# A decoder layer with a mixture of experts: VectorE's routing of the first two batches split in two, the rest of it moved to the end of a loop step

## The reference

```python
x = x + _layernorm(_L0_attn_ref(_layernorm(x), ...))     # 16 heads of 128, causal, rotary, gated keys and values
x = x + _layernorm(_L0_ffn_ref(_layernorm(x), ...))      # 8 experts, 2 per token, and a shared MLP
```

```python
logits = jnp.einsum('td,de->te', x_flat, router)         # 2048 tokens, 8 experts
topk_logits, sel = jax.lax.top_k(logits, K)              # K = 2
cw = jax.nn.softmax(topk_logits, axis=-1)
C = int(np.ceil(T * K / E * CAP_FACTOR))                 # 640 slots per expert
e_flat = sel.reshape(-1)
oh = jax.nn.one_hot(e_flat, E, dtype=jnp.int32)
pos_all = jnp.cumsum(oh, axis=0) - oh                    # how many earlier choices took the same expert
pos = jnp.take_along_axis(pos_all, e_flat[:, None], axis=1)[:, 0]
valid = pos < C
buf = jnp.zeros((E, C, d)).at[e_flat, safe_pos].set(x_flat[tok], mode='drop')
```

## Time and profile before

| | |
|---|---|
| median of the runs | 801.26 us (799.38 to 807.01) |
| profiled execution: its span | 801.3 us |
| granted TensorE clock, mean | 0.988 |
| TensorE busy | 746.7 us, 93% |
| VectorE busy | 599.3 us, 75% |
| GpSimd busy | 560.1 us, 70% |
| ScalarE busy | 500.0 us, 62% |

### The profile page before, as it was taken

One profiled execution on the slowest core, in us unless ns is written; L12 is line 12 of the kernel. 1 busy time (PEld: TensorE's weight loads), 2 busy tenths in 40 slices (PEclk: granted clock), 3 DMA queues, 4 the chain that ended last, 5 costly groups with the idle time before them and its releaser, 6 DMA issues.

```text
span 801.3 us, 14115 instructions
## 1 busy us (share of the span) xinstructions
PE 746.7 (93%) x4364; PEld 626.4 (78%) x4364; DVE 599.3 (75%) x1590; ACT 500.0 (62%) x1171; POOL 560.1 (70%) x465
## 2 busy tenths in 40 slices
PE   5899999999999999999989999999899988899992
PEld 4677788888888888887768888778678888898761
DVE  6658876768898877889977888998662457775675
ACT  5778777786777677666657766667523255553432
POOL 4777988888889887787869988789533534433653
PEclk9999999999999999999989999999999999999996
DMA  9312245422222221221122222112151144542332
GB/s 312 116 40 63 90 150 181 146 70 67 66 68 67 67 67 67 66 67 55 61 60 80 83 77 66 55 60 70 58 153 47 56 147 172 187 144 89 109 95 90
DMA packets 47733, 75.74 MB, mean 95 GB/s; under 512 B 9712, under 2 KB 24624, under 8 KB 47664
## 3 DMA queue, kind: packets, MB, share of 16 engines
q1 hardware_dynamic: 43504, 65.19, 25.5%
q0 software_dynamic: 3072, 8.39, 3.3%
q10 hardware_dynamic: 1088, 1.31, 0.5%
HBM read 57.71 MB, written 17.17 MB: 93 GB/s over the span
## 4 chain that ended last, share of the span: by engine, by line
PE 68%; DVE 9%; POOL 8%; issue 7%; ACT 6%; DMA 2%; DVEq 0%; another core or an unknown queue 0%; ACTq 0%; POOLq 0%
PE ps L430 19%; PE ps L976 14%; PE ps L941 13%; PE ps L992 9%; PE ps L962 7%; PE ps L1138 3%; POOL o_lo L1778 2%; POOL q_sw L1764 1%; POOL q_sw L1756 1%; POOL kh_row L1773 1%; POOL q_lo L1768 1%; POOL slot_inputs L1794 1%; ACT prob L643 1%; ACT y_sb L856 1%; DVE hid_both L1652 1%
## 5 line engine op out<-in xcount | busy, mean ns | idle before, releaser
L643 ACT ACTIVATE prob<-ps,neg_max 128x512 f32<-128x512 f32 (+3 forms) x256 | 132.5, 526 | 75.3 <-DVE neg_max L1321 75.2
L976 PE MATMUL ps<-pt,vp 128*128 128x512 f32 (+3 forms) x512 | 150.0, 436 | 8.0 <-issue 6.4
L976 PEld LDWEIGHTS ps<-pt,vp 128*128 128x128 f32 x512 | 83.0, 191 | 57.4 <-issue 26.4
L1321 DVE CUSTOM_DVE_ANT_0 ps<-ps,causal_row 128x512 f32<-128x512 f32 (+3 forms) x256 | 117.3, 520 | 0.0
L1778 POOL TENSOR_TENSOR o_lo<-o_t,o_hi 128x512 fp32r<-128x512 f32 x64 | 87.1, 1361 | 35.5 <-ACT o_hi L671 34.6
L1768 POOL TENSOR_TENSOR q_lo<-q_sw,q_hi 128x512 fp32r<-128x512 f32 x62 | 83.1, 1340 | 39.5 <-ACT q_hi L665 39.2
L962 PE MATMUL ps<-id_f,prob 128*128 128x128 f32 x640 | 92.5, 275 | 2.3 <-ACT pt L652 2.3
L941 PE MATMUL ps<-k_hi,q_hi 128*128 128x512 f32 x248 | 87.4, 352 | 3.8 <-issue 3.2
L1764 POOL TENSOR_TENSOR q_sw<-q_cos,q_sw 128x512 f32<-128x512 f32 x62 | 79.0, 1273 | 15.6 <-DVE q_cos L1313 7.4
L1334 DVE TENSOR_SCALAR pt<-ps,vcol 128x384 f32<-128x384 f32 (+2 forms) x192 | 82.3, 476 | 9.5 <-PE ps L962 9.5
L1756 POOL TENSOR_TENSOR q_sw<-q_sw,rope_sb 128x512 f32<-128x512 f32 x64 | 82.1, 1283 | 2.6 <-ACT q_sw L632 1.9
(11 more groups left out here) (219 smaller groups left out, 1946.7 us busy)
## 6 DMA issues: line engine op xcount, KB each, us to landing
kh_row<-kvh_rows SPq DMA_DIRECT2D x64, 256.0 KB, 3.1
inv_row<-inverse_sums SPq DMA_DIRECT2D x64, 256.0 KB
slot_inputs<-zeros SPq DMA_DIRECT2D x8, 640.0 KB, 4.8
xg<-slot_inputs SPq DMA_DIRECT2D x8, 640.0 KB, 4.6
slot_outputs<-yo SPq DMA_DIRECT2D x8, 640.0 KB, 3.3
up_raw<-in_w_up_dram SPq DMA_DIRECT2D x8, 368.0 KB, 4.8
wo_raw<-in_wout_dram SPq DMA_DIRECT2D x4, 512.0 KB, 7.8
dn_sb<-in_w_dn_dram SPq DMA_DIRECT2D x8, 256.0 KB, 3.7
```

The lines of the kernel that those rows point to most:

```text
L643: ins = act.activation(prob[:, i % 2, ROW_AT[nt]:ROW_AT[nt] + w], ps_s[bank][:, at:at + w], ACT.Exp, scale=-1.0, bias=neg_max[:, i % 2, nt ...
L976: ins = pe.matmul(ps_qo[:, mt * P:SEQ], vp[:, b * TPB + mt, :], pt[:, i % 2, cols], start=(mt == 0), stop=(mt == PT_BANKS[-1][-1]))
L1321: ins = dve.tensor_tensor_reduce(s_, s_, causal_row[:, (NT - 1 - nt) * P:], 1.0, BIG, ALU.add, ALU.min, neg_max[:, i % 2, nt:nt + 1])
```

## The change

The functions `best_experts` and `find_slots` are each split: their first part, which waits for TensorE and copies the bank out, becomes `take_logits` and `take_positions`, and stays where it was. The rest of `best_experts`, all of `choose` and the rest of `find_slots` are called at the end of the same step of VectorE's loop, after `rest_of_keys(i + 3)`. For batches 2 and 3 the two parts are called one after the other, so their order is as before.

```diff
-            def best_experts(g):
-
-                logit, top, top_at = tables[g][0:3]
+            def take_logits(g):
+                logit = tables[g][0]
                 dve.wait_ge(token_psum, g + 1)
                 bank, at = TOKEN_AT[g]
                 turned = ps[bank][:, at:at + TPB * 32].rearrange("p (t c) -> p t c", t=TPB)
                 done(dve.tensor_copy(logit[:], turned[:, :, 0:NE]))
                 dve.sem_inc(token_taken, 1)
+
+            def best_experts(g):
+
+                logit, top, top_at = tables[g][0:3]
                 for t in range(TPB):
                     ins = dve.max(top[:, t, :], logit[:, t, :])
...
-            def find_slots(g):
-
-                top_f, oh, pos_sb, pos_oh, slot, slot_in = tables[g][3:]
-                ts = group_tiles(g)
+            def take_positions(g):
+                pos_sb = tables[g][5]
                 dve.wait_ge(pos_psum, g + 1)
                 done(dve.tensor_copy(pos_sb[:].rearrange("p t e -> p e t"),
                                      ps[TOKEN_AT[g][0]][:, POS_AT:POS_AT + TPB * NE].rearrange("p (e t) -> p e t", e=NE)))
                 dve.sem_inc(pos_taken, 1)
+
+            def find_slots(g):
...
                     elif n == TURN_LOGITS + 1:
                         if b:
                             dve.wait_ge(kh_scaled, 3 * H - PLAIN)
-                        best_experts(b)
-                    elif n == TURN_LOGITS + 2:
-                        choose(b)
+                        take_logits(b)
                     elif n == POSITIONS + 1:
-                        find_slots(b)
+                        take_positions(b)
...
                 if i + 3 < UNITS:
                     rest_of_keys(i + 3)
+                for b, n in routes(i):
+                    if n == TURN_LOGITS + 1:
+                        best_experts(b)
+                    elif n == TURN_LOGITS + 2:
+                        choose(b)
+                    elif n == POSITIONS + 1:
+                        find_slots(b)
                 if i == UNITS - 3:
```

More of the change, by code:

```diff
@@ L1474, in find_slots @@
                 dve.sem_inc(pos_taken, 1)
+            def find_slots(g):
+                top_f, oh, pos_sb, pos_oh, slot, slot_in = tables[g][3:]
+                ts = group_tiles(g)
                 for k in range(2):
@@ L1592, in _ @@
                 normalize_y(B - 1, t)
+            take_logits(ROUTED)
             best_experts(ROUTED)
@@ L1596, in _ @@
             shared_hidden(0, [0, 1])
+            take_positions(ROUTED)
             find_slots(ROUTED)
@@ L1610, in _ @@
             shared_hidden(2, [0])
+            take_logits(B - 1)
             best_experts(B - 1)
@@ L1613, in _ @@
             shared_hidden(2, range(1, SH))
+            take_positions(B - 1)
             find_slots(B - 1)
```

## The result

The changed kernel takes **807.87 us** (median of 8 runs, 804.61 to 811.81) against 801.29 us for the kernel before (8 runs, 798.78 to 807.01). The ratio is 1.0073 with a 95% interval of 1.0043 to 1.0104 (the two medians divided give 1.0082, inside it): slower by 3 to 8 us, inside the forecast range and within the 1% of "same", but clear of no change at all. The forecast was 802. Its picture of where TensorE would stand idle holds; two terms of the sum are too small, and it started from a span that is above the median of before. It also booked as a gain, in full, a loss that some executions of the kernel before probably don't have; that is likely, but not shown.

What follows compares the result with a forecast made beforehand. It took TensorE to bound the kernel, with time won or lost only where it stands idle around the routing. Stalls of 6.8 us per batch, 13.6 against 13.0 before, gave 801.3 + 0.6 = 802 us; range 794.5 to 810.

Steps and rivals of the forecast that it cites:

- Step 38, cost 0: With `choose` gone from this gap, q_cos fits by 0.3 us; cost 0 now, 1.61 us before.
- Step 39, 1.5 us with its tail: `choose` now stands ahead of this step's q_cos: TensorE idle 1.36 us, 1.5 us with the clock tail of 0.14.
- The sign that `gap` would take over 1 us: In VectorE's timeline, `gap`, an instruction of `choose`, was to last over 1 us, almost all waiting for GpSimd.
- The sentence that `positions` is covered: In step 39 TensorE's `positions` waits for `choose`, but `choose` ends over 1 us before q_cos, so no added cost.
- Step 40, cost 0: The rest of `find_slots` leaves this gap, so q_cos is in time; cost 0 now, 1.78 us before.
- Step 41, 5.0 us: The rest of `find_slots` meets the four statistics: 2.8 us idle plus 2.2 us of halved clock; bounds 1.6 to 6.5 us.
- The sign of a slot_in over 1 us: In VectorE's timeline, slot_in, a small instruction of `find_slots`, was to last over 1 us.
- The 5.45 us of k_lo come back: In batch 0, late q_cos of step 41 leaves GpSimd idle before o_lo, k_lo gets in, and its 5.45 us loss goes.
- the second rival: k_lo is still held off in step 41 for one batch: 807.4 us, chance 0.11.
- the rule of the shared port: VectorE and GpSimd take turns, first holding the port one whole instruction; k_lo would wait 1.3 us, its 6.16 speaks against.
- the first: Rival: small VectorE instructions fit beside GpSimd; step 39 costs 0, step 41 1.78 us; 792.4 us, chance 0.13.
- the third rival: k_lo is held off in step 40 when o_lo starts without a break, 5.45 us per batch: 812.9 us, chance 0.10.

Runs made afterwards that it cites:

- a3: The changed kernel with the four statistics of x moved one step later, directly ahead of the second `variances`; 803.35 us, ratio 1.0032 to the kernel before.
- d1_probes: The kernel before with three 8-element additions added in step 27 and three BN_STATS in step 29, each waited for; 801.27 us in one execution.
- b1: The kernel before with the first scatter in step 43 (59) and the others one step later or in the next; 801.24 us, ratio 0.9998.
- c1: The kernel before with y_back of the third tile, half of `find_slots` and the statistics of x moved to a later step; 801.39 us, ratio 0.9996.
- d2: The kernel before with the same instructions laid so that no gap holds more than two that wait for GpSimd; 800.49 us, ratio 0.9990.
- a1_choose_only: The changed kernel with only `choose` still moved and the two other groups back in their old place; 805.09 us, ratio 1.0038 to the kernel before.

## Why the prediction was right, and where not

- *What bounds the kernel*: right. All of the difference is idle time of TensorE and clock lost behind it.
- *Step 38, cost 0*: right. q_cos starts at 366.41 (366.3 forecast) and the weighing comes 7.96 us after the one before.
- *Step 39, 1.5 us with its tail*: measured 2.06 us longer than a plain step, less 0.19 for `positions`, so 1.87; 2.11 in batch 1. `choose` took 3.93 us (372.09 to 376.02) and not the 3.07 of its old place. The sign that `gap` would take over 1 us did not come: it took 0.15 us, and the sentence that the cost is 0 without its wait was wrong, because chosen and counts, 0.23 and 0.22 us before, now took 1.2 us each, a turn apiece. The sentence that `positions` is covered was wrong too: it waits 1.00 and 1.22 us for `choose`. The two waits run one after the other, so this only moved the idle time. In the timeline of VectorE after:

```profile
372.09 0.15 DVE L1452 TENSOR_TENSOR gap<-top 128x4 f32<-128x4 f32 x1
...
373.67 1.21 DVE L1460 TENSOR_TENSOR chosen<-oh 128x32 bf16<-128x32 f32 x1
374.92 1.19 DVE L1461 TENSOR_TENSOR_SCAN counts<-same_expert,chosen 128x32 bf16<-128x32 bf16 x1
```

- *Step 40, cost 0*: right.
- *Step 41, 5.0 us*: the term that was mis-sized most. Measured: 4.09 and 3.86 us in step 41 and 57, and 2.78 and 1.46 us of slower clock in the step after, so 6.9 and 5.3 us. The gap was summed with `find_slots` at the 3.61 us of its old place. There the copy of the bank came first, and GpSimd stopped for q_cos after three instructions. In its new place it started earlier against GpSimd, during q_lo, so it had one instruction more to sit out, and took 5.57 us. The sign of a slot_in over 1 us did not come either (0.17 us); keep waited instead. That the clock would go at the 2.8 us of the sum was never measured, since the idle times were 4.00 and 3.77 us; a3 shows that 2.2 us already cost clock.
- *The 5.45 us of k_lo come back*: right in both traces of the changed kernel (no k_lo over 2.5 us in any step), and it was 6.1 us. In the timed runs of before it can hardly have been there each time: the earliest start of weighing 35 (342.9), the stretch of the loop with it (236.7) and the shortest rest behind weighing 63 in any trace (220.8) make a span of 800.4 us, and 17 of 32 runs of before have a span below that, down to 795.1. This takes for granted that the start and the rest don't get shorter than in the 14 traces, which no run shows. So the sum counted as a gain in full what the median of before perhaps only partly pays. It is a likely cause of what is left between the traces (4 us) and the medians (6.6 us, interval 3 to 8), but not a shown one; how many of the timed runs have it was not measured, since only one execution in each set has a trace.
- *The sum and the range*: in the traces the routing of both batches loses 13.66 us before and 16.78 after, against 13.0 and 13.6 in the sum. So 0.6 us were forecast for this part and 3.1 measured, and 6.6 between the medians. That 807.87 lies in the range is partly luck: the range reached to 810 to take in the second rival (807.4 us), which is not what happened.
- *Against the rule of the shared port* that the Trainium skill states (the section cited above): the additions of the probe went by it, and the sum had been better off to take it further than one example, and count turns. keep, with one SBUF input, waited too in one trace and not in another. Only k_lo, with 512 columns, was passed over by several instructions of GpSimd. The prediction's own sentence, that k_lo does not get in while GpSimd goes straight on, was too strong: in step 40 of the changed kernel it took 1.02 us and q_lo, which followed without idle time, 1.76 instead of 1.30, so k_lo got in between.
- *The rivals*: none came about. Of the first, `gap` was indeed not held up, but the small instructions after it were. k_lo was not held off in steps 40 and 41 of the changed kernel; for step 40 this was close, since GpSimd went from q_lo into o_lo with no idle time, the sign that the third rival named, and k_lo was in by then.

## What to carry to other kernels

Work moved from ahead of a deadline in one loop step to the end of that step stands ahead of the same deadline of the next one; look at what it meets there. Where VectorE and GpSimd work side by side, cost a run of small VectorE instructions with two SBUF inputs by the number of GpSimd instructions they have to sit out and not by their own durations. And a trace of one execution can hold a loss that another execution does not have: k_lo of step 41 took 6.2 us in the three traces of before and 3.8 in d1_probes, which has the same routing. The other way round, b1, c1 and d2 are 3 to 6 us shorter in the routing of their traces and the same in their medians. Their traces also start the routing 1.2 to 4.8 us later than the first trace of before, and why their medians show no gain stays open: a gain in one stretch of one trace is not yet a gain in time.

## What the runs showed of the hardware

- Three VectorE additions of 8 elements, each waited for, lasted 3.30 us beside GpSimd, 1.1 us each; three BN_STATS of 256 columns lasted 1.31 us beside it.
- A two-input VectorE instruction of 512 columns (k_lo) lasted 0.7, 1.6, 2.3, 3.8 or 6.2 us with the same operands. In those of 6.2 us GpSimd went from one instruction into the next with no idle time until it stopped for q_cos. Instructions of 4 to 32 columns did get in at such places, and k_lo did so as well in step 40 of the changed kernel (1.02 us), step 43 of b1 (2.32) and step 41 of d1 (3.77). What decides it is not shown.
- The granted clock fell to 0.50 after idle times of 4.00 and 3.21 us, and was low after 2.34 us as well (0.57 in the stretch behind it). After 1.4 to 1.9 us it mostly stayed at 1.00, but in a1_choose_only it fell after 1.12 and 0.55 us, in step 54 of d1_probes after 1.66 us (0.61 in the stretch behind it), and near the end of the loop after 1.59 us in one of two traces of the changed kernel and after 1.60 us in c1_spread.
